# Mamba-2 layer and ternary feed-forward on Trainium2: the next slice's quantization moved behind the current slice's activation, with a rotation of three PSUM tiles

## The reference

```python
def _quantize(w):
    gamma = jnp.mean(jnp.abs(w))
    return jnp.clip(jnp.round(w / (gamma + EPS)), -1.0, 1.0)
def _bitlinear(x, w):
    return jnp.matmul(x, _quantize(w).T)
x1 = _bitlinear(x, w1)
x2 = _bitlinear(x, w2)
hidden = jax.nn.sigmoid(x1) * x2
return _bitlinear(hidden, w3)

x = x + _L0_attn_ref(_layernorm(x, axis=-1), ...)
x = x + _L0_ffn_ref(_layernorm(x, axis=-1), L0_ffn_w1, L0_ffn_w2, L0_ffn_w3)
```

## Time and profile before

| | us |
|---|---|
| runs | 6650.16 and 6933.44 |
| median of the two | 6791.8 |
| profiled execution | 6650.16 |
| its span, slowest core (6) | 6648.6 |
| spans of the eight cores | 6609.0 to 6648.6 |
| granted TensorE clock, mean of the core | 0.771 of full |

### The profile page before, as it was taken

The page is one execution under the profiler, slowest core; times in us unless marked ns, Lnnn a source line. Parts: engine busy times, 40 slices in busy tenths (PEclk is TensorE's granted clock), DMA queues, the critical chain, the costliest instruction groups (busy, mean ns, idle before and its releaser), DMA issues.

```text
span 6648.6 us, 59546 instructions; the slowest of 8 cores (6609.0 to 6648.6 us)
## 1 busy us (share of the span) xinstructions
PE 4564.0 (69%) x21030; PEld 2254.9 (34%) x21348; DVE 2311.2 (35%) x2673; ACT 1500.2 (23%) x1611; POOL 549.6 (8%) x1090
## 2 busy tenths in 40 slices
PE   3775666785663565665746439777788565799998
PEld 0333555431221222222322114455553222344443
DVE  2776555431223121212212227655531222211112
ACT  1233333322003424233242111233322101000000
POOL 0001222100000000000000000123210000000000
PEclk8895555796775787887878769755578677899999
DMA  3892000581322434233242404100023231222222
GB/s 87 220 251 99 27 27 27 149 225 35 67 57 70 145 106 148 105 123 134 94 168 93 161 15 76 30 2 2 2 49 54 57 67 29 82 76 77 76 76 83
DMA packets 144887, 577.02 MB, mean 87 GB/s; under 512 B 36947, under 2 KB 39252, under 8 KB 106580
## 3 DMA queue, kind: packets, MB, share of 16 engines
q1 hardware_dynamic: 76468, 398.76, 17.9%
q0 software_dynamic: 68128, 174.44, 12.1%
HBM read 589.57 MB, written 85.98 MB: 102 GB/s over the span
## 4 chain that ended last, share of the span: by engine, by line
PE 56%; DVE 16%; DMA 14%; ACT 9%; issue 4%; POOL 1%; DVEq 0%; ACTq 0%; SPq 0%; POOLq 0%
PE p_ip L1035 10%; PE p_ip L1044 9%; PE p_ip L893 8%; PE p_ip L274 6%; PE p_ip L829 4%; PE p_ip L1071 4%; PE p_w L1071 4%; DMA aW_w2slab<-w3T_t 4%; PE p_ip L723 3%; DMA aX_gslab<-w3T_t 3%; DVE aW_woslab L877 2%; DMA aX_gslab<-w1T_t 2%; DVE aW_tscr L375 1%; PE p_ip L284 1%; DVE STATES_bf L377 1%
## 5 line engine op out<-in xcount | busy, mean ns | idle before, releaser
L1035 PE MATMUL p_ip<-aH_h,aW_q 128*128 128x512 bf16 x2761 | 703.9, 416 | 771.0 <-ACT aW_sig L1051 638.3
L893 PE MATMUL p_ip<-aA_xy,aW_woslab 128*128 128x512 bf16 x2006 | 524.0, 426 | 267.7 <-DVE aW_woslab L877 264.4
L1035 PEld LDWEIGHTS p_ip<-aH_h,aW_q 128*128 128x128 bf16 x2816 | 293.1, 105 | 1174.9 <-issue 903.2
L1044 PE MATMUL p_ip<-aH_h,aW_q 128*128 128x512 bf16 x2760 | 618.9, 379 | 3.0
L274 PE MATMUL p_ip<-aW_stageR,aW_stageL 2*128 2x128 f32 x2048 | 511.2, 427 | 42.7 <-DMA aW_eacsrow<-aW_eacs 42.4
L274 PEld LDWEIGHTS p_ip<-aW_stageR,aW_stageL 2*128 2x128 f32 x2048 | 471.5, 325 | 104.8 <-issue 88.5
L723 PE MATMUL p_ip<-aH_h,aW_wslab 128*128 128x512 bf16 x1504 | 367.3, 403 | 167.8 <-DMA aW_wslab<-winT_t 72.5
L893 PEld LDWEIGHTS p_ip<-aA_xy,aW_woslab 128*128 128x128 bf16 x2048 | 217.5, 107 | 574.2 <-issue 385.8
L1044 PEld LDWEIGHTS p_ip<-aH_h,aW_q 128*128 128x128 bf16 x2816 | 275.6, 98 | 332.1
L1071 PE MATMUL p_w<-aA_hid,aA_q3l 128*128 128x512 bf16 x1371 | 333.3, 380 | 45.0 <-DVE aW_outstg L1083 22.8
L1071 PE MATMUL p_ip<-aA_hid,aA_q3l 128*128 128x512 bf16 x1386 | 333.9, 380 | 12.9 <-DVE aW_outstg L1083 11.0
(11 more groups left out here) (162 smaller groups left out, 6486.6 us busy)
## 6 DMA issues: line engine op xcount, KB each, us to landing
aW_wslab<-winT_t POOLq DMA_DIRECT2D x92, 512.0 KB, 6.2
aX_gslab<-w1T_t SPq DMA_DIRECT2D x44, 1024.0 KB, 7.7
aX_gslab<-w2T_t SPq DMA_DIRECT2D x44, 1024.0 KB, 7.0
aX_gslab<-w3T_t SPq DMA_DIRECT2D x44, 1024.0 KB, 8.7
aW_w1slab<-w1T_t SPq DMA_DIRECT2D x44, 1024.0 KB, 9.1
aW_w2slab<-w2T_t SPq DMA_DIRECT2D x44, 1024.0 KB, 6.0
aW_w2slab<-w3T_t SPq DMA_DIRECT2D x44, 1024.0 KB, 5.7
aW_woslab<-woutT_t POOLq DMA_DIRECT2D x32, 1024.0 KB, 8.3
```

Source lines behind the costliest of these rows:

```text
L893: ev_mm = P.add(T, lambda t, par=par, lh=lh, ec=ec, pb=pb: t.matmul(pb[lh][:, :], B["woslab"][par][:, 128 * ec:128 * ec + 128], B["xy"][:, ...
L1035: ex1 = P.add(T, lambda t, par=par, lh=lh, k=k: t.matmul(B["p_Y"][lh][:, :], B["q1"][par][:, 128 * k:128 * k + 128], B["h1"][:, k, 512 * l ...
L1044: ex2 = P.add(T, lambda t, par=par, lh=lh, k=k: t.matmul(B["p_diff"][lh][:, :], B["q2"][par][:, 128 * k:128 * k + 128], B["h1"][:, k, 512 ...
```

## The change

`quantall(li)` is now called at the head of slice li's turn, behind the sigmoid and the product of slice li - 1, and the call ahead of the loop is gone. x1 and x2 no longer have PSUM tiles of their own: the three tiles `p_ip[0..2]` are taken in turn, x1 in tile a, x2 in the next, and the next slice starts two further on. `pipf` holds what frees each tile. Since `p_sh` is half of `p_ip[2]`, the W3 groups that use it also wait for what last read tile 2, and the tile's list gets the last W3 read of `p_sh`.

```diff
--- before.py
+++ after.py
@@ -952,8 +952,10 @@
         q2f = [None, None]
         q3lf = [None] * FFN_R
         hidf = [None] * FFN_R
-        x1pf = {0: pfree["p_Y0"], 1: pfree["p_Y1"]}
-        x2pf = {0: pfree["p_diff0"], 1: pfree["p_diff1"]}
+        pipf = [[pfree["p_Y0"], pfree["p_Y1"]],
+                [pfree["p_diff0"], pfree["p_diff1"]],
+                [pfree["p_sh"], pfree["p_small"]]]
+        pcyc = [0]
         w3pf = [pfree["p_w3"], pfree["p_sh"]]
         sigf = None
         qtmpf = [None]
@@ -1022,39 +1024,42 @@
                 q3_ready[li] = eq3
                 return eq1, eq2, eq3
 
-            pend = quantall(0)
             for li, hc in enumerate(rnd):
                 par = li % 2
-                eq1, eq2, eq3 = pend
+                eq1, eq2, eq3 = quantall(li)
+                a_i = pcyc[0]
+                b_i = (a_i + 1) % 3
+                pcyc[0] = (a_i + 2) % 3
+                px1 = B["p_ip"][a_i]
+                px2 = B["p_ip"][b_i]
                 ex1 = ex2 = None
                 for lh in range(2):
                     for k in range(16):
                         w = [ev_h2k[k]]
                         if lh == 0 and k == 0:
-                            w = w + [eq1, x1pf[0], x1pf[1]]
-                        ex1 = P.add(T, lambda t, par=par, lh=lh, k=k: t.matmul(
-                            B["p_Y"][lh][:, :], B["q1"][par][:, 128 * k:128 * k + 128],
+                            w = w + [eq1] + pipf[a_i]
+                        ex1 = P.add(T, lambda t, par=par, lh=lh, k=k, px1=px1: t.matmul(
+                            px1[:, 512 * lh:512 * lh + 512], B["q1"][par][:, 128 * k:128 * k + 128],
                             B["h1"][:, k, 512 * lh:512 * lh + 512],
                             start=(k == 0), stop=(k == 15)), waits=w)
                 for lh in range(2):
                     for k in range(16):
                         w = []
                         if lh == 0 and k == 0:
-                            w = [eq2, x2pf[0], x2pf[1]]
-                        ex2 = P.add(T, lambda t, par=par, lh=lh, k=k: t.matmul(
-                            B["p_diff"][lh][:, :], B["q2"][par][:, 128 * k:128 * k + 128],
+                            w = [eq2] + pipf[b_i]
+                        ex2 = P.add(T, lambda t, par=par, lh=lh, k=k, px2=px2: t.matmul(
+                            px2[:, 512 * lh:512 * lh + 512], B["q2"][par][:, 128 * k:128 * k + 128],
                             B["h1"][:, k, 512 * lh:512 * lh + 512],
                             start=(k == 0), stop=(k == 15)), waits=w)
                 q1f[0] = q1f[1] = ex1
                 q2f[0] = q2f[1] = ex2
-                pend = quantall(li + 1)
-                es2 = P.add(A, lambda a: a.activation(B["sig"][:, :], B["p_ip"][0][:, :], AF.Sigmoid, scale=0.5),
+                es2 = P.add(A, lambda a, px1=px1: a.activation(B["sig"][:, :], px1[:, :], AF.Sigmoid, scale=0.5),
                             waits=[ex1, sigf])
-                x1pf = {0: es2, 1: es2}
-                eh2 = P.add(V, lambda v, li=li: v.tensor_tensor(
-                    B["hid"][:, li, :], B["sig"][:, :], B["p_ip"][1][:, :], ALU.mult),
+                pipf[a_i] = [es2]
+                eh2 = P.add(V, lambda v, li=li, px2=px2: v.tensor_tensor(
+                    B["hid"][:, li, :], B["sig"][:, :], px2[:, :], ALU.mult),
                     waits=[es2, ex2, hidf[li]] + (mam_bar if ri == 0 and li < 2 else []))
-                x2pf = {0: eh2, 1: eh2}
+                pipf[b_i] = [eh2]
                 sigf = eh2
                 hid_ready[li] = eh2
             for dc in range(16):
@@ -1066,7 +1071,8 @@
                         w = []
                         if li == 0:
                             w = [w3pf[pw_i], q3_ready[-1], hid_ready[-1]] + (
-                                [q3_ready[-2]] if len(rnd) > 1 else [])
+                                [q3_ready[-2]] if len(rnd) > 1 else []) + (
+                                pipf[2] if pw_i == 1 else [])
                         ev_mm = P.add(T, lambda t, dc=dc, lh=lh, li=li, pwb=pwb,
                                       st_=(li == 0), sp_=(li == len(rnd) - 1): t.matmul(
                             pwb[:, :], B["q3l"][:, li, 128 * dc:128 * dc + 128],
@@ -1092,10 +1098,13 @@
             for li in range(len(rnd)):
                 hidf[li] = ev_last_w3
                 q3lf[li] = ev_last_w3
+            pipf[2] = pipf[2] + [w3pf[1]]
         pfree["p_w3"] = w3pf[0]
-        pfree["p_sh"] = w3pf[1]
-        pfree["p_Y0"] = pfree["p_Y1"] = x1pf[0]
-        pfree["p_diff0"] = pfree["p_diff1"] = x2pf[0]
+        pfree["p_Y0"] = pfree["p_Y1"] = pipf[0][0]
+        pfree["p_diff0"] = pfree["p_diff1"] = pipf[1][0]
+        pfree["p_sh"] = pfree["p_small"] = w3pf[1]
+        for e_ in pipf[2]:
+            pfree["p_sh"] = e_ if pfree["p_sh"] is None else pfree["p_sh"]
 
     P.add(G, lambda g: g.engine_nop(), waits=out_dma_evs)
     P.emit()
```

## The result

| | before | changed |
|---|---|---|
| median of all executions, us | 6829.72 (13; 6634.4 to 6992.22) | 6474.15 (14; 6319.62 to 6667.77) |
| those in which the two halves of the chip (cores 0 to 3, 4 to 7) stay within 1% of each other, us | 6634 to 6661 (6) | 6320 to 6370 (7, six of them below 6331) |
| ratio changed / before | | 0.953, 95% interval 0.9505 to 0.9554 |

A forecast was written before the change was run, and what follows sets the result against it. PE waited for the sigmoid queued behind the Signs; afterwards the w2slab loop would bind. Gains of 211 us (rounds 2 to 5), 59.6 (round 1) and 29.2 (round 6), less 3, took 6650.2 to 6353 us; 80% range 6280 to 6470.

The forecast's parts named there:

- The forecast is for executions like the profiled one.: Whole run: 6353 us applies to executions like the profiled 6650.2 us; the median of two shown was 142 us more.
- The turn of 24.6 us: Segment 0, from one w2 load to the next: mean of six rounds' free-running stretches, slice 0 to slice 1.
- The wait of rows 1 goes: Segment 0: x1's wait for the previous slice's sigmoid, 38 times, 638.3 us of PE idle time, disappears.
- The loop of `w2slab` becomes the bound: Segment 0: loads, Signs and sums of w2 and w3 sharing one buffer take 24.6 us, against PE's 18.8.
- The sigmoid and the product are hidden: Segment 0: sigmoid (1.02 us) and product (1.22 us) run where ACT and DVE have room, without lengthening the buffer loop.
- W3 and the start of the next round: Round ends in segment 0: unchanged, since the q1 sum is behind W3's additions on DVE in both kernels.
- 3 us for segment 1: Rounds 3 and 6: first x1 waits for W3's last addition on tile 2, 1.54 us each, 3 us added.
- Rival 1: Segment 0: PE runs whole slices at half clock, turns of 31 us, run ends near 6665 us; chance 4%.
- Rival 2: Segment 0: the exposed loads stretch moderately under more traffic, run between 6470 and 6540 us; chance 9%.
- Rival 4: Segment 0: buffer loop not binding, all 638 us won, 6012 us; milder form with shorter loads 6273; chance 5%.
- The range: Whole run: 80% between 6280 and 6470 us, from shorter loads to loads about 3 us a turn longer.

The follow-up runs named there:

- the fastest version: Changed kernel plus w3's own buffer, w1's part of quantall issued between sigmoid and product, and two qtmp buffers taken in turn: 5964.17 and 5969.6 us, ratio 0.898.

## Where the forecast was right and where it failed

The forecast had the mechanism right, but not the time that the median over all executions would take. Two steps of it failed.

- *"The forecast is for executions like the profiled one."* This is the step that puts the measured 6474.15 outside 6280 to 6470. It set the distance from the profiled execution to a median over many at nothing, though it named 142 us for it itself, half of the distance between the two times shown (6650 and 6933). Measured, seven of the changed kernel's 14 executions took 6320 to 6370 us and seven 6579 to 6668, and the median is 146 us above 6328. What makes one execution of the same kernel that much longer stays open; no experiment here bears on it. That the median fell only 4 us outside is chance: with one more short execution it would have been 6370 or less, with one more long one near 6579.
- *The turn of 24.6 us.* This is the term of the sum that was mis-sized. It measured 23.6, worth 32 us of gain that the sum left out, while 6353 lies 25 us above 6328; W3's later and slower start took part of it back.

Point by point:

- *The wait of rows 1 goes.* Right. The trace shows no x1 behind a sigmoid.
- *The loop of `w2slab` becomes the bound.* Right, and shown by edits: the turn moves with the w3 load alone (half of w3: 22.0 us), falls to 17.6 us once the buffer is split, and is the same with two tiles or three (23.5 and 23.6).
- *The sigmoid and the product are hidden.* Right; they start at the places named, and the two Sign groups of the loop keep their 5.56 us.
- *The turn is 24.6 us.* It measured 23.6. The term took the free-running turns from slice 0 to slice 1, where the w2 load of before was long: 7.34 us in the earlier trace rows. The stage's own medians in the trace of before, 6.0 us for w2 and 5.7 for w3, were not used:

```profile
aW_w2slab<-w3T_t SPq DMA_DIRECT2D x44, 1024.0 KB, 5.7
aW_w1slab<-w1T_t SPq DMA_DIRECT2D x43, 1024.0 KB, 9.1
aW_w2slab<-w2T_t SPq DMA_DIRECT2D x43, 1024.0 KB, 6.0
```

  With these the 24.11 us of round 3 would have been 24.11 - 12.59 + 11.7 = 23.2, nearer to the 23.6 measured but below it. On 32 turns (six in each of five rounds, two in the last) 24.6 instead of 23.6 is 32 us of gain left out. The w3 load, 5.25 us in one row, was 6.0, so the two loads were wrong in opposite directions, and by that luck the turn came out only 1.0 us too long. Why the w2 load of slice 1 took over 7 us in all six rounds of before, and mostly 5.7 to 6.5 us on core 0 after the change, is not settled and was not tried.
- *W3 and the start of a round stay.* Nearly. The way to W3 is 20.5 us instead of the 19.7 forecast, and W3's own block 2.2 us longer in round 3, by its slow start behind 4.16 us of idle time. The forecast had no term for that. PE waited 18.8 us in front of the six W3 blocks.
- *3 us for segment 1.* Measured 1.12, twice, in the two rounds named.
- *Rival 1, half clock in whole slices.* It did not come. In round 3 x1 began slowly behind each gap of 7 us or more (8.8 to 9.6 us), x2 ran in 7.07 each time, and the round's clock rose from 0.82 to 0.87. The rule in the Trainium skill ("TensorE: Matmul & The Clock Gate", A second HAM failure mode) would have had the rotation over three tiles bring the slow clock; the granted clock with the rotation and without it is the same here, 0.785 on core 0 of the changed kernel and 0.786 on core 0 with the moved call alone.
- *Rival 2, slower loads.* The traffic rose to 155 GB/s, as worked out (153), and the w2 and w3 loads stayed within 0.3 us of their medians before. Loads as long as the 8.7 us of the earlier trace rows came at such traffic again: in the fastest version, at 275 GB/s, w2 and w3 landed in 8.7 and 9.0 us, where it did no harm. The Trainium skill's fit ("DMA: Bandwidth & Descriptors", Anatomy of one DMA) is stated there for transfers that go by POOL, while these loads are on SP's queue. The estimate of 4.4 us for 1 MB that was worked out from it is below every median here.
- *Rival 4, all of rows 1.* It needs the split buffer, as the forecast said. With it the kernel ended at 6075; with the chain through `qtmp` opened too, at 5964, under the 6012 of the rival. There x1 also loses most of its slow starts, 7.07 us for some 9, and that on 38 slices is an estimated 73 us.
- *The range.* It was built for executions like the profiled one and holds those (6320 to 6370). For the median over all of them it had no term, as said above.

## What to carry to other kernels

When a wait goes, look for the loop that is next: a buffer shared by two loads is such a loop, and its pace can be read where it already runs free. Read that pace with the median of all its loads, not with those of one place. And when the times of one kernel shown lie 4% apart, say where in between the forecast number is to fall, or make the range as wide. Two edits that free the same link (move the call, rotate the tile) do not add up. Those that free different links do: 318 us for the call, 263 for the buffer of w3, 569 for both. So the next gain comes from the link that the first one left, here 253 us for 1 MB of buffer and 108 more for a scratch buffer and an earlier sum.

## What was not expected of the hardware

- The length of a gap in front of a matmul group did not by itself decide its speed, for gaps of 2.3 to 3.3 us. 2.35 us in front of the first x1 of a round left 32 matmuls at 7.07 us in round 3, where before 2.45 us gave 8.75. Of the changed kernel's W3 blocks one started at full speed behind 3.02 us and one at reduced speed behind 2.66:

```profile
2530.45 3.37 PE L1077 MATMUL p_w<-aA_hid,aA_q3l 128*128 128x512 bf16 x8 [2.66 <-DVE aA_hid L1059]
...
3258.54 1.89 PE L1077 MATMUL p_w<-aA_hid,aA_q3l 128*128 128x512 bf16 x8 [3.02 <-DVE aA_hid L1059]
```

- Halving a 1 MB load took 1.0 us off the median of 6.0, and 1.5 us off a mean of 6.4 from issue to Sign. By an estimate in a straight line from these means, 3.5 of the 6.4 us do not depend on the bytes, so in this kernel one load fewer in the loop (6 us) was worth far more than one of half the size.
- In the fastest version all eight cores moved 247 to 305 GB/s each between 2300 and 2420 us of their spans, with their DMA engines 75 to 94% busy, and landings of 8 to 9 us were hidden once they overlapped.
